# Attention kernel on one core: four key tiles of each second half turned by VectorE and a trip through DRAM, instead of by TensorE

## The reference, cut to what matters

```python
# x: (2, 1024, 512); 32 query heads of 128, 8 key/value heads; weights are 4-bit integers with scales
xn = layernorm(x)
q, k, v = (xn @ dequant(qw, scales)) ...          # q and k are rotated (RoPE)
scores = einsum('bhqd,bhkd->bhqk', q, k) / sqrt(128)
scores = where(causal, scores, -max)
attn = softmax(scores)                             # f32
ctx = einsum('bhqk,bhkd->bhqd', attn, v)
x + dequant_matmul(ctx, qw_o, scales_o) + lora_ffn(xn)
# lora_ffn: base linear 512x512 + bias + top-2 of 8 rank-16 adapters
```

## Time and profile before

| | us |
|---|---|
| median of 3 executions | 2106.51 (2105.98 to 2108.94) |
| the profiled execution, its time | 2108.06 |
| its span, first to last instruction | 2106.3 |
| mean granted TensorE clock | 0.998 |

### The profile page before, as it was taken

One profiled execution on the slowest core, in us unless ns is written; L12 is line 12 of the kernel. 1 busy time (PEld: TensorE's weight loads), 2 busy tenths in 40 slices (PEclk: granted clock), 3 DMA queues, 4 the chain that ended last, 5 costly groups with the idle time before them and its releaser, 6 DMA issues.

```text
span 2106.3 us, 31748 instructions
## 1 busy us (share of the span) xinstructions
PE 2084.7 (99%) x11690; PEld 1806.4 (86%) x11692; DVE 1510.7 (72%) x3056; ACT 993.5 (47%) x2199; POOL 1213.4 (58%) x1117
## 2 busy tenths in 40 slices
PE   8999999999999999999999999999999999999999
PEld 6888888888888888888888888888888888888887
DVE  6757776777767777677767777677776777767776
ACT  3145454554544545454444445454544545445453
POOL 3745665556655566456664666555665656646542
PEclk9999999999999999999999999999999999999999
DMA  6522222322312233232363422222231224313112
GB/s 222 156 41 61 58 69 56 61 56 56 81 46 57 59 61 76 44 67 58 61 149 80 114 59 63 49 71 61 56 78 34 71 46 79 73 31 70 36 41 66
DMA packets 160923, 145.88 MB, mean 69 GB/s; under 512 B 26368, under 2 KB 117248, under 8 KB 160256
## 3 DMA queue, kind: packets, MB, share of 16 engines
q1 hardware_dynamic: 157312, 137.80, 28.3%
q0 software_dynamic: 2112, 4.19, 0.6%
q10 hardware_dynamic: 1344, 1.85, 0.3%
HBM read 133.06 MB, written 10.75 MB: 68 GB/s over the span
## 4 chain that ended last, share of the span: by engine, by line
PE 94%; DVE 3%; POOL 1%; issue 1%; ACT 1%; DMA 0%; SPq 0%; DVEq 0%; POOLq 0%
PE ring L1123 43%; PE ring L1253 20%; PE O_ps L1123 19%; PE turned L1264 11%; POOL rope L683 1%; DVE rope L991 0%; POOL Q_low L691 0%; DVE rope L993 0%; DVE PT_low L924 0%; DVE stats L880 0%; DMA Y<-in_x 0%; DVE rope L992 0%; PE turned L1168 0%; ACT Q_high L736 0%; DVE xnT_low L924 0%
## 5 line engine op out<-in xcount | busy, mean ns | idle before, releaser
L736 ACT ACTIVATE PT_high<-turned 128x512 fp32r<-128x512 f32 (+3 forms) x771 | 359.2, 488 | 516.1 <-PE turned L1264 496.1
L790 ACT ACTIVATE probs<-probs,negmax 128x128 f32<-128x128 f32 (+7 forms) x512 | 398.1, 777 | 229.6 <-DVE negmax L1002 222.5
L924 DVE TENSOR_TENSOR PT_low<-turned,PT_high 128x512 fp32r<-128x512 f32 (+3 forms) x771 | 410.5, 555 | 117.0 <-ACT PT_high L736 108.6
L1002 DVE CUSTOM_DVE_ANT_0 probs<-ring,mask_row 128x128 f32<-128x128 f32 (+7 forms) x512 | 386.0, 754 | 83.1 <-PE ring L1253 74.2
L698 POOL TENSOR_TENSOR ctx_low<-ctx_f,ctx_high 128x512 fp32r<-128x512 f32 x128 | 165.4, 1292 | 410.0 <-ACT ctx_high L736 410.0
L1264 PE MATMUL turned<-ident,probs 128*128 128x128 f32 x2304 | 344.5, 273 | 0.0
L683 POOL TENSOR_TENSOR rope<-rope 128x512 f32<-128x512 f32 x160 | 206.9, 1293 | 177.0 <-DVE rope L993 175.9
L1264 PEld LDWEIGHTS turned<-ident,probs 128*128 128x128 f32 x2304 | 273.2, 140 | 35.5
L1123 PE MATMUL O_ps<-PT_high,V_high 128*128 128x512 f32 (+3 forms) x768 | 284.9, 371 | 7.1 <-DVE PT_low L924 7.1
L1043 DVE TENSOR_TENSOR Y<-ring,Y 128x512 f32<-128x512 f32 x256 | 177.0, 692 | 126.0 <-PE ring L1123 121.8
L1123 PE MATMUL O_ps<-PT_high,V_low 128*128 128x512 f32 (+3 forms) x768 | 265.9, 346 | 0.0
(11 more groups left out here) (115 smaller groups left out, 3861.1 us busy)
## 6 DMA issues: line engine op xcount, KB each, us to landing
R_sb<-row_sums SPq DMA_DIRECT2D x128, 256.0 KB, 4.1
raw<-in_qw_q SPq DMA_DIRECT2D x64, 256.0 KB, 4.8
scl<-in_scales_q SPq DMA_DIRECT2D x64, 256.0 KB, 8.6
raw<-in_qw_o SPq DMA_DIRECT2D x64, 256.0 KB, 4.5
scl<-in_scales_o SPq DMA_DIRECT2D x64, 256.0 KB, 4.8
raw<-in_qw_k SPq DMA_DIRECT2D x16, 256.0 KB, 4.5
scl<-in_scales_k SPq DMA_DIRECT2D x16, 256.0 KB, 6.1
raw<-in_qw_v SPq DMA_DIRECT2D x16, 256.0 KB, 4.4
```

What stands on the lines that cost most here:

```text
L736: return nc.scalar.activation(dst, src, ACT.Copy)
L790: nc.scalar.activation(probs[:, at], probs[:, at], ACT.Exp, bias=negmax[:, i:i + 1], scale=-1.0, accum_out=sums[:, i:i + 1]).then_inc(exp_ ...
L924: nc.vector.tensor_tensor(out=dst, in0=src, in1=high.bitcast(f32), op=ALU.subtract).then_inc(pt_low, 1)
L1002: nc.vector.tensor_tensor_reduce(probs[:, prob_at[i]:prob_at[i] + n], score_place(u, h, i), mask_row[:, TOKENS - n:TOKENS], -1.0, -MASKED, ...
```

## The change

Half 1 of a head no longer turns key tiles 0 to 3 on TensorE. Instead:

- `scores` for tiles 4 to 7 reads its first 512 keys in another order (the moving operand is a rearranged view), so that a row of `probs` has keys b*32+k of the four tiles j side by side: b, j, k. The two matmuls of such a score now cover 512 and the remaining 128 to 512 columns; before they were two equal halves.
- DVE transposes the 512 first columns of each of these four rows of tiles in place, as squares of 32x32 (`turn_squares`).
- SP stores each of the four (256 KB, `move_out`) to DRAM, and when all four have landed loads them back with four DMAs (`move_in`, 256 KB each), in runs of 128 elements (512 bytes), so that partition blocks and column blocks change places. `moved` then has the turned tiles.
- ACT makes the high part (`moved_tile_high`, two buffers) and POOL, not DVE, the low part (`moved_tile_low`).
- Half 1 sums its tiles in the order 4, 5, 0, 1, 6, 7, 2, 3 (VALUES). `PT_low` has two buffers, `PT_high` three.

The rest of the change: all eight scores of the next head now stand in half 1 of the head before it (before: four there, four in half 0 of the head itself). Half 0 has the projections and outputs. The inverse row sums are fetched right after the place R_sb is free (`divided`), no more at a fixed place. To make room in SBUF, `raw` has one buffer instead of two, the second term of the rotation (`rope_b`) has one, and the weights have 9 slots instead of 11: q2 shares with q0 and q3 with k. The offsets of most instructions in the queues change too.

```diff
-FIRST = "T F V O S S S T S T T V O V V"
-FIRST_P = "F P P T S O T T V S T V S P V S O P V"
-EARLY = "S T T F V S T V S S T O O V V"
-THIRD = "T S F T V S T S S T V V O O V"
-LATE = "S T T T S F V T V T V O V T T V T S S O V T V V V"
+FIRST = "T F V F O T O T T O V V O"
+FIRST_P = "F P T O T F P P O V P T O O V T V V"
+EARLY = "F T F V T O T O O T V O V V"
+THIRD = "F F T F T O O V T O V T F O V V"
+LATE = "S T S T S T S V V S V T V S V S V S V V"
...
+VALUES = ([0, 1, 2, 3], [4, 5, 0, 1, 6, 7, 2, 3])
+MOVED = 4
...
             def load_weight(u, w):
                 n = weight_number[u, w]
-                if n >= 2:
-                    if seen.new(w_done, n - 1):
-                        sp.wait_ge(w_done, n - 1)
+                if n:
+                    if seen.new(scaled, n):
+                        sp.wait_ge(scaled, n)
...
+            def move_out(u, h, i):
+                n = head_of(u, h)
+                if seen.new(squared, 4 * n + i - 3):
+                    sp.wait_ge(squared, 4 * n + i - 3)
+                if n > 1:
+
+                    if seen.new(moved_in[n % 2], 64 * (n // 2)):
+                        sp.wait_ge(moved_in[n % 2], 64 * (n // 2))
+                sp.dma_start(squares[n % 2][i - 4].rearrange("p (b n) -> p b n", b=4),
+                             row_squares(i).rearrange("p (b n) -> p b n", b=4)).then_inc(moved_out[i - 4], 16)
+
+            def move_in(u, h):
+                n = head_of(u, h)
+                for i in range(4):
+                    if seen.new(moved_out[i], 16 * (n + 1)):
+                        sp.wait_ge(moved_out[i], 16 * (n + 1))
+                if n:
+
+                    if seen.new(moved_done, 4 * n):
+                        sp.wait_ge(moved_done, 4 * n)
+                back = squares[n % 2].rearrange("r (a k) (b n) -> b k (r a) n", a=4, b=4)
+                for b in range(4):
+                    sp.dma_start(moved[32 * b:32 * (b + 1), :, :, :].rearrange("p t j q -> p t (j q)"),
+                                 back[b]).then_inc(moved_in[n % 2], 16)
...
-            weights, sums = weights_due(STEPS, -8.0), behind(STEPS, 1.0, "turn")
-            sums_there = behind(STEPS, 4.0, "turn")
...
+            weights, sums = weights_due(STEPS, -8.0), behind(STEPS, 4.0, "scores")
+            divided, sums_there = behind(STEPS, 1.2, "values"), behind(STEPS, 9.3, "scores")
+            squares_out, squares_in = behind(STEPS, 3.0, "scores"), behind(STEPS, 5.8, "scores")
...
+                nc.gpsimd.tensor_tensor(out=low, in0=moved[:, :, j, :], in1=high.bitcast(f32),
+                                        op=ALU.subtract).then_inc(moved_done, 1)
...
+            moved_due = [behind(STEPS, us, "scores") for us in (13.4, 14.0)]
+            multiplied = behind(STEPS, 0.1, "values")
...
+                copy(moved_high[:, j % 2, :].rearrange("p (t q) -> p t q", t=16),
+                     moved[:, :, j, :]).then_inc(moved_high_done, 1)
...
+            moved_due = [behind(STEPS, us, "scores") for us in (13.5, 17.6)]
+            multiplied = behind(STEPS, -0.2, "values")
...
+            def turn_squares(u, h, i):
+                need = score_number[u, h, i]
+                if seen.new(exp_done, need):
+                    dve.wait_ge(exp_done, need)
+                nc.vector.transpose(row_squares(i), row_squares(i)).then_inc(squared, 1)
...
-                ps, a, b = place(step), rope_a[:, n % 2, :], rope_b[:, n % 2, :]
+                ps, a, b = place(step), rope_a[:, n % 2, :], rope_b
                 nc.vector.tensor_tensor(out=a, in0=ps, in1=cos_sb[:, half(c)], op=ALU.mult)
+                if n > 1:
+                    if seen.new(rope_sum, n - 1):
+                        dve.wait_ge(rope_sum, n - 1)
...
-                banks = [(0, cut)] + ([(cut, n)] if n > cut else [])
...
+                        moving = keys[:, lo:hi]
+                        if i >= 4 and lo == 0:
+
+                            moving = moving.rearrange("p (j b k) -> p b j k", j=MOVED, b=4)
```

More of the change, by code:

```diff
@@ L43 @@
[L43 to L56 removed]
+WEIGHT_SPAN = 112.0
@@ new lines @@
+LATE = "S T S T S T S V V S V T V S V S V S V V"
+LAST = "T S S T V S V T V V S S V T S S V V V S"
+LAST_P = "S T S T V P S T V T V S V S S P P V S V S P V V"
+VALUES = ([0, 1, 2, 3], [4, 5, 0, 1, 6, 7, 2, 3])
+MOVED = 4
+def parts(u):
+    q = lambda v, h: [("project", v, f"q{h}", c) for c in range(2)]
+    out = lambda u, p, c: [("output", u, p, 4 * c + t) for t in range(4)]
+    projected, outputs = [q(u, 1), [], q(u, 2), [], q(u, 3), [], [], []], [[] for _ in range(2 * REP)]
+    for c in range(2):
+        outputs[2 * c] = out(u - 1, 1, c) if u else []
+        outputs[4 + 2 * c] = out(u, 0, c)
@@ L117, in tensor_order @@
     steps += [("project", 0, w, c) for w in ("k", "q0") for c in range(2)]
-    steps += [("rows_v", 0, t) for t in range(NT)]
-    steps += [("scores", 0, 0, i) for i in range(4)]
+    steps += [("rows_v", 0, t) for t in VALUES[1]]
+    steps += [("scores", 0, 0, i) for i in range(NT)]
     for u in range(UNITS):
@@ L128, in weight_order @@
     for u in range(UNITS):
-        order[u] = [(u, w) if w[0] == "o" else (u + 1, w) for w in (PREPARED if u else PREPARED_FIRST)
-                    if w[0] == "o" or u + 1 < UNITS and (w[0] != "v" or u % 2)]
+        order[u] = [(u, w) if w in OWN else (u + 1, w) for w in (PREPARED if u else PREPARED_FIRST)
+                    if w in OWN or u + 1 < UNITS and (w[0] != "v" or u % 2)]
     return order
@@ L149, in begins @@
             t = max([t] + [acted[s[1], s[2], 4 * s[3] + q] for q in range(4)])
+        elif s[0] == "values" and s[4] < 4 * s[3]:
+            t = max(t, acted[s[1], s[2], 7] + 15.0)
         at.append(t)
@@ L251, in build_program @@
     turn_number = numbers(*TURNED)
+    slot_number = {("values", *s[1:]): n for n, s in enumerate(s for s in STEPS if s[0] == "turn")}
+    slot_reader = {n: s for s, n in slot_number.items()}
+    valued_number = {s: n + 1 for n, s in enumerate(s for s in STEPS if s[0] == "values" and s[4] != VALUES[s[3]][-1])}
     score_number = {s[1:]: n for s, n in numbers("scores").items()}
@@ L922, in low @@
                     dve.wait_ge(pt_high, turn_number[step])
+                if step[0] == "turn" and slot_number["values", *step[1:]] >= LOWS:
+                    reader = slot_reader[slot_number["values", *step[1:]] - LOWS]
+                    if reader in valued_number:
+                        if seen.new(valued, valued_number[reader]):
+                            dve.wait_ge(valued, valued_number[reader])
+                    else:
+                        need = head_number[reader[1:4]]
+                        if seen.new(o_full, need):
+                            dve.wait_ge(o_full, need)
                 high, dst, src = split_of(step)
@@ L1252, in scores @@
                     for lo, hi in banks:
-                        mm = nc.tensor.matmul(ps[:, lo:hi], lhs[:, tile], keys[:, lo:hi], start=first, stop=last)
+                        moving = keys[:, lo:hi]
+                        if i >= 4 and lo == 0:
+                            moving = moving.rearrange("p (j b k) -> p b j k", j=MOVED, b=4)
+                        mm = nc.tensor.matmul(ps[:, lo:hi], lhs[:, tile], moving, start=first, stop=last)
                 mm.then_inc(ring_full, 1)
@@ L1268, in values @@
             def values(u, h, c, j):
-                has_turned("turn", u, h, c, j)
+                step = ("values", u, h, c, j)
+                if j >= 4 * c:
+                    has_turned("turn", u, h, c, j)
+                elif seen.new(moved_done, 4 * head_of(u, h) + j + 1):
+                    pe.wait_ge(moved_done, 4 * head_of(u, h) + j + 1)
                 if seen.new(v_low, value_number[u - u % 2, j]):
                     pe.wait_ge(v_low, value_number[u - u % 2, j])
-                if j == 0:
+                first, last = j == VALUES[c][0], j == VALUES[c][-1]
+                if first:
                     n = head_number[u, h, c]
@@ L1276, in values @@
                             pe.wait_ge(ctx_made, n - 1)
[L1277 removed]
                 at = slice(max(0, j - 4 * c) * P, HALF)
[L1279 to L1283 removed]
+                if j < 4 * c:
+                    turned_tile = moved_high[:, j % 2, :], moved_low[:, j % 2, :]
+                else:
+                    slot = slot_number[step]
+                    turned_tile = PT_high[:, slot % TURNS, at], PT_low[:, slot % LOWS, at]
+                mm = product(O_ps[:, at], [(both(V_high, V_low, slice(None), u % 2, j), turned_tile)],
+                             start=first, stop=last)
+                mm.then_inc(o_full if last else valued, 1)
             def output(u, p, t):
```

246 lines of the change are left out of this document (156 added, 90 removed).

## The result

| | us |
|---|---|
| before, median of 4 executions | 2106.49 (2105.98 to 2108.94) |
| after, median of 4 | 2268.76 (2263.62 to 2284.17) |
| ratio | 1.0785, 95% interval 1.0739 to 1.0831 |
| after, the profiled execution and its span | 2284.17, 2282.4 |
| mean granted TensorE clock, before and after | 0.998, 0.949 |

A forecast was written before the change was run, and what follows sets the result against it. TensorE, issuing back to back, was taken as the bound: 2108.1 - 112.6 + 5.8 = 2001.3 us, plus 19 us of new waits, less 1.5 us to the median, gave 2018 us; range 1995 to 2066.

The forecast's parts named there:

- Transposes off PE: Half 1 on TensorE: 1024 transposes fewer at 0.110 us each, 112.6 us off; 282 us by the skill's figure.
- the new cut of the scores: TensorE's scores of tiles 4 to 7, cut 512 + rest: only tile 4 dearer, 5.8 us on.
- DVE: 256 transposes at 0.69 us (other bound 0.96) replace 256 `PT_low` subtractions: net nothing, at the edge in half 1.
- POOL: 256 low parts at 1.293 us add 331 us, to 1544 us busy; up to half more for runs of 32.
- 19 us for everybody's new waits: All engines' new waits: 0.3 us a head, between 0 and one late POOL instruction per head (83 us).
- rival B: POOL paces the kernel: a further 0.6 to 1.2 us a head, 2040 to 2075 us; chance 0.22.
- ACT: 256 copies at 627 ns replace 256 at 596 ns: 8 us more, counted as nothing; late transfers hold up turns.
- The transfer: Squares' trip through DRAM: back 15.5 us after the last score, ceiling 22, against 18 us available.
- The landing: Last return's landing after the last score: 5.8 + 1.8 + about 3 + 4.9 = 15.5 us.
- The deadline: First use of a moved tile on PE, some 20 us after the last score, 18 less ACT's and POOL's copies.
- Rival D: Squares back late: decides at 19.7 us after last score; 2130 to 2255 us; sign: PE waiting for `moved_low`; chance 0.11.
- DMA traffic: 4096 more packets a head, DMA busy 60 to 80% of the span; weights land later, POOL waits for them.

The follow-up runs named there:

- e12: Kernel after without stores and returns, copies reading the cosine table, POOL's low parts cut to 32 of 512 columns, TensorE reading high parts instead: 2024.9 us.
- e2: Kernel after without stores and returns of the squares; the moved copies read the cosine table without waiting: 2068.8 us.
- e18: Kernel after with a copy of the scales of q and k for each of the 128 partitions, at the old pitch: 2065.7 us.
- the halves: Kernel after with scales and integers of q and k by head, and returns issued in two halves: 2057.4 us, ratio to before 0.9742.
- e19: Kernel after with the scales of q and k padded by 64 columns, to a pitch of 16,640 bytes for q: 2127.6 us.
- e4: Kernel after with ACT's and POOL's copies of moved tiles 0 and 1 placed later, ACT's at 17.3 and 17.6 us behind the last score: 2264.4 us.
- e9: Kernel after summing the moved tiles last, half 1's steps reordered, copies 19 to 21 us behind the last score: 2240.7 us.
- e3: Kernel after with weight loads held back on SP until a head's returns are issued: 2335.3 us.
- e17: Kernel after with the four rows of a head's scales 576 bytes apart: 2087.8 us.
- e1: Kernel after with all stores and returns kept, but the moved copies read the cosine table, so nobody waits for the trip: 2124.0 us.
- e13: Kernel after with the scales of q and k laid out by head, one row of 2 KB: 2073.1 us.

## Why the prediction was wrong, point by point

**Transposes off PE, the new cut of the scores:** right. e12's busy time is 1982.2 against 1977.9 worked out. The 112.6 us, taken from the distance of the starts, stand; 282 us would have put e12 169 us lower, near 1856 us, and it took 2025.

**DVE:** right. 705 ns a transpose with 5.8 us of waits in all, near the lower of the two bounds.

**POOL:** the price of one (1.286 us; runs of 32 elements cost nothing) and the busy sum (1523.7 for 1544) were right, its lateness was too small: 19 us for everybody's new waits, where e2 less e12 gives 44 us, clock included. That is rival B's size (0.6 to 1.2 us a head). It would have brought 2018 to 2043, inside the range. How much of it would be left beside fast scales no run shows (e12 has the slow ones).

**ACT:** 629 ns and nothing else was wrong. The sentence on the turns that stand behind a late transfer was there, with no price.

**The transfer is the step that failed:** "15.5 us fits with 2.5 us to spare, and the ceiling misses by 4". Both sides of that comparison were off:

*The landing.* Mean 18.1 and median 17.5 us for 15.5, with a tail that reaches 23.6 us. The terms are means of the 64 heads, worked out from the records of the instructions and the landings; e18 is the same kernel with mended scales:

| us | forecast | after | e18 |
|---|---|---|---|
| start of the row maximum to the first issue | 5.8 | 8.3 | 7.3 |
| of these: landing of the last store | 2.0 | 4.0 | 2.9 |
| first to last issue | 1.8 | 1.9 | 1.5 |
| last issue to last landing | 7.9 | 7.9 | 6.2 |
| sum | 15.5 | 18.1 | 15.0 |

The store was priced at 2.0 us from the `out` stores and takes twice that. Nothing else on SP holds the returns up: the first goes out 0.24 us after the last store has landed. Of the 3.1 us between the kernel after and e18, 1.0 is in the stores, 0.4 in the issues and 1.7 in the returns: that is the slow read. That e18 comes near the forecast 15.5 is partly luck, since a first issue that is 1.5 us later than forecast and a return that is 1.7 us shorter cancel. (The 3 us that don't grow with size should have been 4.8 - 1.2 = 3.6 by the prediction's own rows.) I had read the 8.6 us of the scales as a queue ("8.6 less 4.8, scales behind integers"). The row of the W_o scales, same place in the queue and 4.8 us, contradicted that, and I did not read it. The window from which I took 38 ns a packet held a load for k, whose four rows lie 4 KB apart, and none for q.

*The deadline.* I took it at 18 us, from the first use of a moved tile on PE. In the head shown, the wait reaches TensorE through ACT's queue, where the copy was planned at 13.5 us with half 0's `PT_high` behind it, and at a mean delay of 15.0 us ACT already waits 143 us (e18). With the places as in the change, a us of mean delay goes with about one us a head: after less e18 is 203 us / 64 = 3.2 us for 3.1 us of delay, e19 less e18 1.0 for 1.0. The first pair has a second difference, POOL's wait for the scales of q (109.5 us in after, 7.4 in e19, 1.3 in e18), so its 3.2 us are not the delay's alone. The queue's place is not the whole of it: e4 moved it 4 us back and took 2264 us, e9 moved it to 19 us and took 2241. Nor is the delay: e3 brought it down to a mean of 16.4 us and took 2335, with POOL waiting 308.5 us for scales. So 2.5 us to spare is refuted, while what part of the loss is due to ACT's place, to the late tail and to POOL's late scales stays open.

**Rival D** had the right mechanism (back late, slower) and the wrong point: it was to decide at 19.7 us and did so between the mean delays of 15.5 us (e17, 2088 us) and 16.0 (e19, 2128 us), one execution each. Its price, 2130 to 2255, was short of 2269 by 14 us at its upper end. Its sign, PE waiting for `moved_low`, would have missed it: PE waits 14.8 us there and 169.6 us for `PT_low`.

**The clock** was in no term. After less e18 is 218.5 us of span; of these 146 are idle time of PE and 72 more busy time with the same instructions, (2076.3 - 2003.9), which is the stretch at 1.2 GHz behind the long waits: by the clock records PE is busy 180 us at half clock in the kernel after and 33 in e18, and half of the difference is 74.

**DMA traffic** was seen as 60 to 80% of the span and harmless; it was 47.9% and cost 55 us (e1 less e2), by late scales. The sum had 4096 packets a head, and the queue's count rose by (329,344 - 157,312) / 64 = 2688: the 2048 of the returns leave 640 for the stores, where the sum has 2048. With mended scales e18, with traffic and wait, takes 2065.7, no more than e2 with neither and slow scales, 2068.8; what the traffic costs beside fast scales alone no run shows.

Side by side: sum 2001; without POOL's part and the trip, slow scales, 2025; without the trip, slow scales, 2069; the whole change with mended scales 2066 (e18) to 2073 (e13); the whole change with slow scales 2269. So even with fast scales the change takes some 50 us more than the 2018 of the forecast, at and above the upper end of its range, and gains at most 2% until the halves are added. That a buffer less for `raw` adds to POOL's waits was argued, and no run tries it.

## What to carry to other kernels

When two rows of a view that should be alike (scales of q, scales of W_o) differ by a factor of two, settle that before pricing with either: a slow transfer that hides today (nothing was gained by mending it in the kernel before, 2107.6 us) can delay the transfers that are put next to it. Look for a latency's deadline at the place of the waiting instruction in its engine's queue too, and at what stands behind it there, not only at the first use of the data; moving that place is no cure for a late landing (e4, e9). Compare the tail with the deadline and not only the middle. And price a long wait of TensorE (7.5 us here) with the stretch at half the clock that follows.

## What the runs showed of the hardware that was not expected

- 256 KB read as 512 packets of 512 bytes from four rows that 128 partitions share: 9.4 us at a pitch of 16,384 bytes, 5.6 at 16,640, 4.8 at 576; 4.4 us with unshared rows. For k, at pitches of 4,096 and 4,352 bytes, 5.8 and 4.1 us (median of 16 loads). Behind such a load other transfers crawl too: 52 GB/s over 5 us with up to 1 MB queued, against 181 GB/s with the rows 576 bytes apart.
- A DVE transpose of 128x512 in squares of 32, in place, takes 705 ns, and 256 of them waited 5.8 us in all beside a POOL that is busy 67% of the time.
- TensorE behind a wait of 7.5 us: granted clock 0.50, 512-column matmuls 0.43 us apart, back to 1.00 some 4 us after the first of them. Over the run PE's busy time was 72 us longer than in e18 with the same instructions.
